# Where the rounded and low parts of U begin in memory: one place within 256 bytes for all streams, or a place for each

## The reference, cut to what matters

```python
h = relu(layernorm(x)); x = x + L0(h, adj)   # hypergraph conv 256->512, relu, norm, conv 512->256
h = relu(layernorm(x)); x = x + L1(h, adj)   # GCN: tanh(norm(adj) @ (h @ W) + b)
h = relu(layernorm(x)); x = x + L2(h, adj)   # attention over adj: A @ h @ w
h = relu(layernorm(x)); x = x + L3(h, adj)   # three GCN layers: adj @ (h @ W) + b
```

## The kernel before

| tensor | start modulo 256 bytes |
|---|---|
| WHI, WLO (moving in W steps) | 128 |
| UHI, ULO of every stream (stationary in W steps) | 192 |
| SHARES (stationary), BIAS4W, BIAS5W (moving) | 192 |
| SPREAD (stationary), TMP_D (moving; L280, once at the start) | 192 |
| H, H0, Z (stationary in U steps), AE, GZ (moving) | 192 |
| T, AT (moving), HT (stationary, L315) | 64 |
| G_A, G_B, G_C, G_D (moving, 0U; written by ScalarE, L431) | 64, 96, 128, 160 |

## Time and profile before

### The profile page before, as it was taken

The page is one execution under the profiler, slowest core; times in us unless marked ns, Lnnn a source line. Parts: engine busy times, 40 slices in busy tenths (PEclk is TensorE's granted clock), DMA queues, the critical chain, the costliest instruction groups (busy, mean ns, idle before and its releaser), DMA issues.

```text
span 1433.8 us, 34585 instructions
## 1 busy us (share of the span) xinstructions
PE 1392.3 (97%) x10900; PEld 1331.7 (93%) x10900; DVE 1287.9 (90%) x4001; ACT 990.5 (69%) x2312; POOL 947.7 (66%) x1876
## 2 busy tenths in 40 slices
PE   3799999999999999999999999999999999999997
PEld 2799999999999999999999999999999999999996
DVE  5789999999999999999999999999999999999984
ACT  3577777777777777777777777777777777777763
POOL 2676676676676676676676676676676676676652
PEclk9999999999999999999999999999999999999999
DMA  7011110120110110110110110110110110110100
GB/s 187 1 42 27 52 51 26 51 51 26 51 51 26 51 51 26 51 51 26 51 51 26 51 51 26 51 51 26 51 51 26 51 51 26 51 51 26 37 19 23
DMA packets 83078, 62.70 MB, mean 44 GB/s; under 512 B 40304, under 2 KB 65520, under 8 KB 83056
## 3 DMA queue, kind: packets, MB, share of 16 engines
q1 hardware_dynamic: 83056, 62.43, 15.8%
HBM read 45.62 MB, written 16.78 MB: 44 GB/s over the span
## 4 chain that ended last, share of the span: by engine, by line
PE 95%; DVE 2%; ACT 1%; issue 0%; DMA 0%; POOL 0%; SPq 0%; DVEq 0%; POOLq 0%
PE BANK L365 29%; PE BANK L330 24%; PE BANK L372 15%; PE WIDE L365 8%; PE WIDE L341 8%; PE WIDE L372 4%; PE BANK L357 2%; PE BANK L315 2%; PE BANK L384 2%; DMA TMP_D<-in_l2wt 0%; PE WIDE L278 0%; DVE BN_B L550 0%; DVE BN_C L550 0%; ACT UHI_D L444 0%; PE WIDE L284 0%
## 5 line engine op out<-in xcount | busy, mean ns | idle before, releaser
L444 ACT ACTIVATE UHI_B<-BANK 128x512 fp32r<-128x512 f32 x96 | 57.0, 593 | 43.9 <-PE BANK L330 43.9
L444 ACT ACTIVATE UHI_D<-BANK 128x512 fp32r<-128x512 f32 x96 | 57.1, 595 | 41.1 <-PE BANK L330 41.1
L444 ACT ACTIVATE UHI_C<-BANK 128x512 fp32r<-128x512 f32 x96 | 57.0, 594 | 41.0 <-PE BANK L330 41.0
L444 ACT ACTIVATE UHI_A<-BANK 128x512 fp32r<-128x512 f32 x96 | 57.1, 594 | 39.1 <-PE BANK L330 39.1
L599 DVE TENSOR_TENSOR ULO_D<-BANK,UHI_D 128x512 fp32r<-128x512 f32 x96 | 65.2, 680 | 18.7 <-ACT UHI_D L444 18.0
L732 POOL TENSOR_TENSOR LN_A<-MV_A,EPS 128x2 f32<-128x2 f32 x80 | 15.9, 198 | 92.3 <-DVE MV_A L558 92.3
L599 DVE TENSOR_TENSOR ULO_A<-BANK,UHI_A 128x512 fp32r<-128x512 f32 x96 | 65.2, 680 | 12.3 <-ACT UHI_A L444 11.8
L599 DVE TENSOR_TENSOR ULO_C<-BANK,UHI_C 128x512 fp32r<-128x512 f32 x96 | 65.1, 678 | 11.1 <-ACT UHI_C L444 9.3
L599 DVE TENSOR_TENSOR ULO_B<-BANK,UHI_B 128x512 fp32r<-128x512 f32 x96 | 65.7, 684 | 10.4 <-ACT UHI_B L444 8.5
L732 POOL TENSOR_TENSOR LN_D<-MV_D,EPS 128x2 f32<-128x2 f32 x80 | 15.8, 197 | 84.7 <-DVE MV_D L558 84.7
L732 POOL TENSOR_TENSOR LN_B<-MV_B,EPS 128x2 f32<-128x2 f32 x80 | 16.7, 209 | 78.2 <-DVE MV_B L558 78.2
(11 more groups left out here) (500 smaller groups left out, 6009.6 us busy)
## 6 DMA issues: line engine op xcount, KB each, us to landing
X_A<-in_xs SPq DMA_DIRECT2D x16, 256.0 KB, 2.8
X_B<-in_xs SPq DMA_DIRECT2D x16, 256.0 KB, 2.8
X_C<-in_xs SPq DMA_DIRECT2D x16, 256.0 KB, 2.8
X_D<-in_xs SPq DMA_DIRECT2D x16, 256.0 KB, 2.8
out_rows<-O_A SPq DMA_DIRECT2D x16, 256.0 KB, 2.0
out_rows<-O_B SPq DMA_DIRECT2D x16, 256.0 KB, 2.1
out_rows<-O_C SPq DMA_DIRECT2D x16, 256.0 KB, 2.1
out_rows<-O_D SPq DMA_DIRECT2D x16, 256.0 KB, 2.1
```

Source lines behind the costliest of these rows:

```text
L444: nc.scalar.activation(UHI[s][:, 0:J * D], bank(s, step)[:, :], ACT.Copy).then_inc(sem(f"c{step}"), 1)
```

## The change

`UHI` and `ULO` of each stream are allocated 64 elements (256 bytes) longer, and used from an element of their own on: 48 (192 bytes) in stream A, 56 (224) in B, 8 (32) in C, 32 (128) in D.

```diff
-        UHI = per_stream("UHI", J * DH, dt=F32R)
-        ULO = per_stream("ULO", J * DH, dt=F32R)
+
+        STARTS = {"A": 48, "B": 56, "C": 8, "D": 32}
+        UHI, ULO = ({s: t[:, STARTS[s]:STARTS[s] + J * DH] for s, t in per_stream(n, J * DH + 64, dt=F32R).items()}
+                    for n in ("UHI", "ULO"))
```

## The result

The changed kernel takes 1448.99 us (1448.78 to 1450.34, 4 runs) where the kernel before takes 1437.33: it is slower. The ratio on record is 1.0095 (95% interval 1.0083 to 1.0107); the two medians are 11.7 us apart, the spans of the two profiled executions 12.9. The forecast was 1430.7, and its range ended at 1444.

The account below looks back on a forecast made before the run. TensorE's matmul starts were taken to bound the kernel. Gains of 6.9 us less 0.5 given back at waits made 6.4, taking the profiled 1435.79 to 1429.4 and the median to 1430.7 us; range 1418 to 1444.

Parts of the forecast that it names:

- what bounds the kernel: TensorE, busy 97% of the span: time is essentially the sum of distances between starts of its matmuls.
- two paces: 256-column W-step matmuls: 276 ns recorded (short) or 281 (long), attributed to two conflicting memory reads; long ones cost 4.4 ns more.
- the direction of the 512-column matmuls of stream A: Step 0W, stream A: wide matmuls get shorter, 394 towards 388 ns; 192 x 6 ns = 1.2 us gained.
- (3): TensorE's W steps read stationary operands at new distances from the moving ones: 6.9 us gained, bounds 16 gain, 9.4 loss.
- half of the long matmuls would become short: 256-column W-step matmuls: 1,300 of 2,600 long ones turn short, at 4.4 ns each, gaining 5.7 us.
- The bias matmuls: Matmuls in 4W and 5W, at distance 0, 6 and 2 ns shorter than 512-column ones at +64; evidence for gains.
- the last part of the prediction: Signs to check after: 276 ns more often than 281; other values would mean the paces belonged to +64 alone.
- (2): ScalarE and VectorE access UHI and ULO at other places: 0, bounds 1.5 us; VectorE has 10% slack.
- (4), the give-back at waits: TensorE's waits for ULO in six 2W and 5W steps of a pass absorb gains: 0.5 us given back.
- Slower: Rival, chance 0.25: the long pace becomes the rule in W steps; at most 9.4 us lost, more likely 4.7.
- No effect: Rival, chance 0.29 including a new deal with the same outcome: the stationary operand's place doesn't choose the pace; 1437 us.
- Far faster: Rival, chance 0.10 within faster's 0.46: conflicts vanish in some streams; one stream of four gives 9 us, about 1424.

Follow-up runs that it names:

- e7_both: Against e2_zero (U at 128 bytes in all streams), weights WHI/WLO moved along too, so the distance is +64 again; ratio to the kernel before 0.9993.
- e13_after_pause_d: Changed kernel plus one tiny GpSimd operation ahead of the bias addition, for stream D alone; 1440.96 us, ratio to the kernel before 1.0003.
- e4_plus32: Changed kernel with UHI/ULO beginning at element 56 in all four streams, distance +32 bytes from the weights; ratio to the kernel before 1.0045.
- e2_zero: Changed kernel with UHI/ULO beginning at element 48 in all four streams, distance 0 from the weights; ratio to the kernel before 1.0109.
- e12_wide: Kernel before with only step 0W's weights moved, by spare columns, so its 512-column matmuls are at distance -64; ratio to the kernel before 0.9975.
- e16_wide_pause: e12_wide plus a tiny GpSimd operation ahead of the bias addition in all four streams; 1415.15 us, ratio to the kernel before 0.9819.
- e17_late_a: Kernel before plus one tiny VectorE operation ahead of stream A's leak (leaky ReLU of the attention scores); ratio to the kernel before 1.0042.
- e14: Changed kernel plus a tiny GpSimd operation ahead of the bias addition in all four streams; 1422.72 us, ratio to the kernel before 0.9877.
- e15: Kernel before plus a tiny GpSimd operation ahead of the bias addition in all four streams; 1416.03 us, ratio to the kernel before 0.9827.
- e6_plus128: Changed kernel with UHI/ULO beginning at element 16 in all four streams, distance +128 bytes from the weights; ratio to the kernel before 1.0055.
- e8_plus160: Changed kernel with UHI/ULO beginning at element 24 in all four streams, distance +160 bytes from the weights; ratio to the kernel before 1.0087.
- e5_plus96: Changed kernel with UHI/ULO beginning at element 8 in all four streams, distance +96 bytes from the weights; ratio to the kernel before 1.0021.

## Why the prediction was wrong

**Right**: what bounds the kernel; that there were two paces and that they came from TensorE's two reads (e7_both); that the durations of the writes to UHI and ULO don't depend on the place (VectorE's L599: 678 to 684 ns before, 679 to 680 after; ScalarE's L444: 593 to 595 before, 593 after); and, of the gains, the direction of the 512-column matmuls of stream A: 233.1 to 230.2 ns between starts, 3 ns for the 6 that I had priced. Their recorded duration, which I said would go towards 388, went from 394 to 393.

**The step that failed first** is what I took in (3): that other distances were "only on the better side", so that half of the long matmuls would become short. It rested on the bias matmuls. For 512 columns the direction held (230.3 ns at 0 for 233.2 at +64); carried over to 256 columns it was wrong, and at a distance of 0 these are the worst of all, 119.2 ns. The bias matmuls were weak ground for 512 columns too, since they differ from those of 0W in what comes before and after them: in e7_both, where they have the same distance in both steps, those of stream A take 398 ns in 4W and 388 in 5W (medians). (The 6 ns of which I wrote are two fifths of 15, not a third; nothing hangs on it.) The two paces belonged to +64 alone, which the last part of the prediction had named as a way to be wrong. Where my sum had 5.7 us of gain, the gross price of the pace is 2.3 ns on some 4,930 matmuls, 11 us, on the wrong side.

**The step that failed second** is (2), VectorE at 0. The durations of the instructions that the change touches did stay. But one VectorE instruction stood 0 to 73 ns away from colliding with GpSimd, and in the changed kernel it comes 2 to 25 ns on the other side. That a few ns on TensorE, hundreds of times, shift the engines against one another by that much is what I take it to be; nothing but places was changed, but the chain from one to the other isn't traced. The row was there before: 423 ns in stream A beside 1,416 to 1,458 in the others, with the same form. I had read the page's VectorE share, 90%, as slack.

**(4), the give-back at waits**, was the right mechanism and works for losses too: in e13_after_pause_d the gross 11 us of pace have shrunk to 3.6 by the spans and to nothing by the ratio, with the holds down from 27.2 to 22.0 us; in e4_plus32 to 6.3 by the medians (holds 27.2 to 22.9). The rest of the shrinking I haven't traced. In the changed kernel the collision brings the holds back to 28.2 us, so that by them nothing is absorbed.

**The rivals.** "Slower" was the sign that came, at 0.25, with the wrong mechanism: not the long pace becoming the rule but paces of 283 and 285 ns beside it, and the collision. Its bound of 9.4 us, and with it the upper end of the range, left both out. "No effect" is refuted as a mechanism by e2_zero and e7_both, though with the collision out it is what e13_after_pause_d shows as the sum. "Far faster" came nowhere: the shortest 512-column matmuls, those of e12_wide and e16_wide_pause, stand at 229.0 and 228.9 ns, 4 ns below those of before, where I had allowed for 15.

**Split of the loss.** Both parts are shown to cost time; how much each has of the 11.7 to 12.9 us isn't settled. By the profiled spans, which are of different comparisons, the collision has 9.3 us and the pace, net of what the waits absorb, 3.6. By the ratios the collision has all of it (1.0095 or 1.0077 with it, 1.0003 without); but the kernel before stood at 1440.56 us in that comparison and at 1436.14 in an earlier one on the same chip, and against the latter 4.8 us would be left for the pace. The two don't simply add either: the collision alone cost 5.2 us in e17_late_a, the pace alone 4.4 to 6.7 between e14 and e15.

**Open**: why the fixed distances give these paces; no model of the memory was tried. And why the kernel before spreads over 1436.8 to 1443.1 us on one chip while e6_plus128 and e8_plus160 keep within 1.4 us there. The race of the leak of A would do it, with margins of 0 to 13 ns in five passes: e5_plus96 and e7_both, which spread over 4.7 and 3.7 us on that chip, have passes with margins of 5 ns or less as well. A mix of the two paces that differs from one execution to the next would do it, too. Only one execution of each was traced.

## What to carry to other kernels

Look in the profile for instructions of one form that take 0.4 us in one place and 1.5 in another: here that was a held port, and with the start times of the two contenders within a few tens of ns an edit elsewhere tipped it. A tiny operation that lets the instruction go first on whose engine others wait was worth more (1.7%) than the best placement of operands (0.25%). Where fp32r matmuls are streamed against the loads of their stationary operands, try the distance of the two operands within 256 bytes, and judge it by the whole kernel: a better or worse pace can be taken back at waits, and can tip a collision elsewhere.

## What the runs showed of the hardware

- The time of an fp32r matmul of 256 columns depends on where its stationary operand lies relative to the moving one, within 256 bytes and down to 16: means from 115.9 to 117.4 ns from start to start at +64 (seven kernels), 119.2 at 0 and 117.0 to 118.7 at the others; for 512 columns from 228.9 at -64 to 233.8 at +96.
- At a distance of +64 bytes there are two paces, 113.4 and 117.8 ns, each kept through whole steps, for 22 and 23 distances in a row; at other distances a pattern that repeats, such as 117, 117, 120 at +48 or 116, 125, 116, 123, 119, 121 at +160.
- The hold of VectorE by GpSimd is decided within 6 ns: a leak that started ahead of the addition took 423 ns, one that started 6 to 139 ns behind it was held, to 1.4 us and more, and in between both occurred (behind by 3 ns 1,576 in the changed kernel, 423 in e4_plus32). The addition holds a VectorE instruction of 2 elements nearly as long (1.2 us).
